# Kept rows turned on VectorE, down weights rounded on ScalarE, and the last 64 features stacked twice

## The reference

```python
s = silu(einsum('bsh,ih->bsi', x, w_gate))
k = int(0.5 * I)                                   # I = 2752
_, idx = jax.lax.top_k(-jnp.abs(s), k)             # the k smallest magnitudes of each row
s[row, idx] = 0
s = s * einsum('bsh,ih->bsi', x, w_up)
return einsum('bsi,hi->bsh', s, w_down)
```

## Time and profile before

| | |
|---|---|
| median of three runs | 1414.09 us (1413.16 to 1414.87) |
| profiled execution | 1414.52 us, span 1412.3 us, mean granted clock 0.99 |
| busy over the span | PE 1367.9 (97%), DVE 981.3 (69%), ACT 739.8 (52%), POOL 942.9 (67%) |
| gate ends, up ends | 851.9 and 1087.8 us |
| down: first matmul, last group from | 1090.9 and about 1280 us |
| chain that ended last | PE 90%, DVE 3%, ACT 2% |

### The profile page before, as it was taken

The page is one execution under the profiler, slowest core; times in us unless marked ns, Lnnn a source line. Parts: engine busy times, 40 slices in busy tenths (PEclk is TensorE's granted clock), DMA queues, the critical chain, the costliest instruction groups (busy, mean ns, idle before and its releaser), DMA issues.

```text
span 1412.3 us, 30485 instructions
## 1 busy us (share of the span) xinstructions
PE 1367.9 (97%) x12727; PEld 1014.2 (72%) x12727; DVE 981.3 (69%) x1324; ACT 739.8 (52%) x935; POOL 942.9 (67%) x613
## 2 busy tenths in 40 slices
PE   4999999999999999899999999999999999999996
PEld 3555555555555555599999998888887888887874
DVE  6888888888888888870001898999997223255654
ACT  6788888888888888732224625243331111111211
POOL 0799888888888888813443342423334899999791
PEclk9899999999999999999999999999999999999998
DMA  9032423233323230024337348383837876865551
GB/s 357 28 103 104 137 98 112 101 115 104 117 100 121 98 107 17 16 77 166 141 123 299 122 163 289 112 286 114 279 120 245 300 256 190 270 191 181 154 192 53
DMA packets 110013, 217.58 MB, mean 154 GB/s; under 512 B 7200, under 2 KB 82864, under 8 KB 104880
## 3 DMA queue, kind: packets, MB, share of 16 engines
q1 hardware_dynamic: 88928, 192.89, 39.6%
q10 hardware_dynamic: 20944, 22.70, 5.2%
HBM read 173.63 MB, written 41.94 MB: 153 GB/s over the span
## 4 chain that ended last, share of the span: by engine, by line
PE 90%; DVE 3%; ACT 2%; DMA 1%; issue 1%; POOL 1%; SPq 0%; DVEq 0%; ACTq 0%; POOLq 0%
PE fast_psum L2002 17%; PE fast_psum L1895 16%; PE fast_psum L2032 15%; PE fast_psum L1913 15%; PE fast_psum L1980 15%; PE fast_psum L1932 6%; PE fast_psum L1939 1%; PE fast_psum L2062 1%; PE fast_psum L2016 1%; PE fast_psum L2083 1%; PE fast_psum L1918 1%; DMA fast_d_raw<-w_down 1%; ACT fast_below L1745 1%; PE fast_psum L1862 1%; ACT fast_g_hi L1717 1%
## 5 line engine op out<-in xcount | busy, mean ns | idle before, releaser
L1321 DVE TENSOR_TENSOR fast_masked<-fast_psum,fast_mask_t 128x1024 f32<-128x1024 f32 (+1 forms) x416 | 488.4, 1219 | 72.2 <-PE fast_psum L1895 70.6
L1177 POOL TENSOR_TENSOR fast_pair<-fast_probs 128x1024 f32<-128x1024 f32 x192 | 457.5, 2386 | 96.1 <-PE fast_psum L1932 47.6
L1658 ACT ACTIVATE fast_probs<-fast_masked 128x1024 f32<-128x1024 f32 (+1 forms) x416 | 438.0, 1058 | 68.6 <-DVE fast_masked L1321 53.6
L1895 PE MATMUL fast_psum<-fast_qT,fast_kraw 32*128 32x256 f32 (+1 forms) x3328 | 247.1, 403 | 6.8 <-ACT fast_qT L1605 3.2
L1913 PE MATMUL fast_psum<-fast_probs,fast_vraw 128*32 128x256 f32 (+1 forms) x3328 | 226.5, 386 | 0.8 <-ACT fast_probs L1658 0.8
L1895 PEld LDWEIGHTS fast_psum<-fast_qT,fast_kraw 32*128 32x128 f32 (+1 forms) x3328 | 153.7, 182 | 93.3 <-DVE fast_masked L1321 53.9
L1232 POOL TENSOR_TENSOR fast_d_lo<-fast_d_raw,fast_d_hi 128x256 fp32r<-128x256 f32 (+1 forms) x264 | 198.4, 781 | 5.3
L1208 POOL TENSOR_TENSOR fast_g_lo<-fast_g_raw,fast_g_hi 128x2816 fp32r<-128x2816 f32 x14 | 87.8, 6273 | 145.6 <-ACT fast_g_hi L1717 123.6
L1980 PE MATMUL fast_psum<-fast_g_hi,fast_z_hi 128*128 128x352 f32 x512 | 165.7, 324 | 1.7 <-POOL fast_g_lo L1208 1.7
L1980 PE MATMUL fast_psum<-fast_g_hi,fast_z_lo 128*128 128x352 f32 x512 | 165.7, 324 | 0.0
L1980 PE MATMUL fast_psum<-fast_g_lo,fast_z_hi 128*128 128x352 f32 x512 | 165.5, 323 | 0.0
(11 more groups left out here) (164 smaller groups left out, 1903.3 us busy)
## 6 DMA issues: line engine op xcount, KB each, us to landing
fast_d_raw<-w_down SPq DMA_DIRECT2D x63, 512.0 KB, 4.0
fast_kraw<-ctx_t SPq DMA_DIRECT2D x32, 800.5 KB, 5.9
fast_vraw<-ctx_nat SPq DMA_DIRECT2D x16, 1536.0 KB
fast_g_raw<-w_gate_up SPq DMA_DIRECT2D x15, 1408.0 KB, 7.3
fast_mag<-s SPq DMA_DIRECT2D x8, 1376.0 KB, 9.8
fast_sx<-s SPq DMA_DIRECT2D x8, 1376.0 KB, 6.7
sk<-fast_sx SPq DMA_DIRECT2D x8, 1376.0 KB, 6.7
fast_u_raw<-w_up_t SPq DMA_DIRECT2D x21, 512.0 KB, 5.0
```

The source lines that it names most:

```text
L1177: pool.tensor_tensor(pair[:, n % PAIR_BUFS], both[:, :, 0, :], both[:, :, 1, :], ALU.add).then_inc(paired, 1)
L1321: dve.tensor_tensor(into, of, m, ALU.add).then_inc(mask_added, 1)
L1658: act.activation(probs[0:r, g % RING, hp * HALF:(hp + 1) * HALF], masked[0:r, h % SLOTS, :], ACT.Exp).then_inc(exp_done, 1)
L1895: last = pe.matmul(scores[0:r, (2 * g + hp) % SLOTS, h % 2, i * 256:(i + 1) * 256], kraw[b % BUFS][q, u, c * P:c * P + r], qT[q, b, u, :], ...
```

## The change

The kept rows are no longer turned by TensorE. VectorE's `keep` writes into `near`, and a new `turn_kept(t)` transposes it in blocks of 32x32 into `sx[t]` (two buffers and, for tile 7, a magnitude buffer). ScalarE's new `store_turned(t)` waits for that and writes the turned blocks with four DMAs to `s_t`, laid out by features; a run there is 32 tokens, 128 bytes. ScalarE's `load_factors(n)` loads from `s_t` and `u_t`, and VectorE's multiply takes both from SBUF. `turn` is gone from TensorE. `near` is held until the transpose is through: `nearest` waits for `sx_turned`. The compares come in two batches of three for each pair.

ScalarE gets the rounding of the down weights, `round_down`: two ahead of the steps, and then `round_down(n + 2)` at the end of stage n. GpSimd keeps the subtraction.

For the last chunk, 64 features, the weights and the factors are loaded twice, on partitions 0 to 63 and 64 to 127. `d_hi` holds the high part on the first half and GpSimd writes the low part over the second, so one matmul over 128 rows makes two products; the third is one of 64 rows.

Core of the diff:

```diff
+        BLK = 32
+        QUARTERS = P // BLK
+        twice = lambda n: n % IC == UF
-        UP_ABS_AT = {6: 4, 12: 5, 19: 6, 25: 7}
-        UP_COUNT_AT = {0: (1, 0), 1: (1, 1), 2: (1, 2), 3: (1, 3), 4: (1, 4), 5: (1, 5),
-                       13: (2, 0), 14: (2, 1), 15: (2, 2), 16: (2, 3), 17: (2, 4), 18: (2, 5),
-                       26: (3, 0), 27: (3, 1), 28: (3, 2), 29: (3, 3), 30: (3, 4), 31: (3, 5)}
+        UP_ABS_AT = {6: 4, 11: 5, 19: 6, 24: 7}
+        UP_COUNT_AT = {0: (1, 0), 2: (1, 3), 12: (2, 0), 14: (2, 3), 25: (3, 0), 27: (3, 3)}
-        UP_SK_AT = {1: 1, 5: 2, 7: 3, 12: 4, 13: 5, 18: 6}
+        UP_SX_AT = {1: 2, 2: 3, 7: 4, 8: 5, 13: 6, 14: 7}
+        GATE_STORE_AT = {62: 0}
+        UP_STORE_AT = {0: 1, 11: 2, 12: 3, 23: 4, 25: 5, 36: 6, 39: 7}
...
             for n in range(STEPS):
-                pool.wait_ge(d_full[j], 16 * (n // DS + 1))
+                pool.wait_ge(d_hi_done, n + 1)
-                pool.tensor_copy(d_hi[j][0:r, :], d_raw[j][0:r, :]).then_inc(d_hi_done, 1)
...
-                    dve.wait_ge(kept, t)
+                    dve.wait_ge(sx_turned, t)
                 done(dve.scalar_tensor_tensor(near, mag[t % MAGS], v, mag[t % MAGS], ALU.is_lt, ALU.mult))
...
-                done(dve.scalar_tensor_tensor(sx, near, thr[:, :], sx, ALU.is_ge, ALU.mult))
+                done(dve.scalar_tensor_tensor(near, near, thr[:, :], sx[t], ALU.is_ge, ALU.mult))
...
+            def turn_kept(t):
+                dve.wait_ge(kept, t + 1)
+                dve.transpose(sx[t], near).then_inc(sx_turned, 1)
...
+            def store_turned(t):
+                act.wait_ge(sx_turned, t + 1)
+                if t == TILES - 1:
+                    act.wait_ge(st_stored[t % 2], 16 * QUARTERS * (t // 2))
+                for q in range(QUARTERS):
+                    act.dma_start(s_t.rearrange("(b r) n -> r b n", r=BLK)[:, :, t * P + q * BLK:t * P + (q + 1) * BLK],
+                                  sx[t][q * BLK:(q + 1) * BLK, :].rearrange("r (b n) -> r b n", n=BLK)
+                                  ).then_inc(st_stored[t % 2], 16)
...
+            def load_factors(n):
                 gi, k = divmod(n, IC)
                 if n >= TURNS:
                     act.wait_ge(h_ready, n - TURNS + 1)
+                if k == 0:
+                    turned = max(GROUPS[gi][-1] + 1, TILES - 2)
+                    for j in range(2):
+                        act.wait_ge(st_stored[j], 16 * QUARTERS * ((turned + 1 - j) // 2))
+                m, t0 = len(GROUPS[gi]), GROUPS[gi][0]
+                act.dma_start(t_s[n % TURNS][0:rows(k), 0:m * P], s_t[k * P:k * P + rows(k), t0 * P:(t0 + m) * P]
+                              ).then_inc(ts_full[n % TURNS], 16)
...
                 if i in UP_ABS_AT:
                     measure(UP_ABS_AT[i])
+                if i in UP_STORE_AT:
+                    store_turned(UP_STORE_AT[i])
                 if i in UP_COUNT_AT:
-                    compare(*UP_COUNT_AT[i])
+                    p, r = UP_COUNT_AT[i]
+                    for r in range(r, r + 3):
+                        compare(p, r)
...
+            def round_down(n):
+                j = n % DS
+                act.wait_ge(d_full[j], 16 * loads(n, DS))
+                if n >= DS:
+                    act.wait_ge(d_done, n + 1 - DS)
+                act.copy(d_hi[j][:, :], d_raw[j][:, :]).then_inc(d_hi_done, 1)
+
+            for n in range(DS - 1):
+                round_down(n)
             for n in range(STEPS):
                 take_high(n)
                 if n + TURNS < STEPS:
-                    load_u(n + TURNS)
-                if n % 2 == 1 and n // 2 + BLOCKS < STEPS // 2:
-                    load_block(n // 2 + BLOCKS)
+                    load_factors(n + TURNS)
...
+                if n + DS - 1 < STEPS:
+                    round_down(n + DS - 1)
...
-            for a, (hp, wp) in enumerate(((h_hi, d_hi), (h_hi, d_lo), (h_lo, d_hi))):
+                products = ((h_hi, d_hi, P), (h_hi, d_lo, P), (h_lo, d_hi, P))
+                if twice(n):
+                    products = ((h_hi, d_hi, P), (h_lo, d_hi, UREST))
```

More of the change, by code:

```diff
@@ L855, in fast, with loads @@
         steps = [0]
+        twice = lambda n: n % IC == UF
+        def loads(n, ring):
+            return sum(2 if twice(m) else 1 for m in range(n % ring, n + 1, ring))
         def u_loads(n):
@@ L1484, in multiply @@
                 gi, k = divmod(n, IC)
-                w, r = len(GROUPS[gi]) * P, rows(k)
-                dve.wait_ge(t_turned, n + 1)
+                w = len(GROUPS[gi]) * P
+                dve.wait_ge(ts_full[n % TURNS], 16 * loads(n, TURNS))
                 if n >= 2:
@@ L1801, in take_high @@
                     act.wait_ge(d_done, n + 1 - HS)
-                act.copy(h_hi[n % HS][0:r, 0:w], t_h[n % 2][0:r, 0:w]).then_inc(h_hi_done, 1)
+                act.copy(h_hi[n % HS][:, 0:w], t_h[n % 2][:, 0:w]).then_inc(h_hi_done, 1)
             def take_zt(t):
@@ L2007, in _ @@
                 up(i)
-            def turn(n):
-                gi, k = divmod(n, IC)
-                q, c = n // 2, n % 2 * P
-                pe.wait_ge(sk_full[q % BLOCKS], 16 * (q // BLOCKS + 1))
-                if n >= 2:
-                    pe.wait_ge(h_ready, n - 1)
-                for i in range(len(GROUPS[gi])):
-                    last = pe.transpose(bank[6 + n % 2][0:rows(k), i * P:(i + 1) * P],
-                                        t_sk[q % BLOCKS][:, i, c:c + rows(k)], eye[:, :])
-                last.then_inc(t_turned, 1)
             def down(n, i):
                 gi, k = divmod(n, IC)
-                r, j, jh = rows(k), n % DS, n % HS
+                j, jh = n % DS, n % HS
                 pe.wait_ge(d_lo_done, n + 1)
```

109 lines of the change are left out of this document (46 added, 63 removed).

## The result

The changed kernel takes 1477.93 us, median of four runs (1471.84 to 1479.24), beside 1414.48 for the kernel before: ratio 1.0445, 95% interval 1.0421 to 1.0469. The profiled execution has a span of 1477.1 us, 64.8 longer. The forecast was 1470, range 1428 to 1530.

A forecast was written before the change was run, and what follows sets the result against it. TensorE was taken to set the time, with VectorE about four us behind in the up stage. From 1414.5 us: + 22 (transposes) + 35 (stores) - 19 (TensorE's work) + 17 (ScalarE's order) = 1469.5, forecast 1470, range 1428 to 1530.

The forecast's parts named there:

- A: Down on TensorE: transposes and the last chunks' third product go, -18.9 us together, all on the path.
- B: Group 2 of down: ScalarE's rounding stands ahead of the factor copies TensorE wants, +17 us, lower bound +5.
- D: Turned-tile stores of 128-byte runs hold ScalarE: 25 us ahead of compares, 10 behind the last store, +35 us.
- 416 descriptor times: One store's four DMAs on ScalarE: total wait for outstanding descriptors; at 20 ns each, a hold of 8.3 us.
- 3 x 8.3: Stores 1, 3 and 5 stand ahead of compares VectorE waits for, each delaying it about 8.3 us: +25.
- rival (2): Short store writes cost 30 to 45 ns a descriptor, holds 12.5 to 19 us; total 1488 to 1550; chance 0.18.
- 9 + 10: From VectorE's last transpose to down's first matmul: 9 us with free issues, 10 more for store 7's held descriptors.
- the limit of about 100 outstanding: DMA issues: an issue is held once about 100 descriptors per DMA engine are outstanding, taken from SyncE's rows.
- C: Eight transposes of about 3.0 us on VectorE in the up stage: VectorE ends near 1104, down starts 22 us later.
- rival (3): VectorE hides the transposes because stretched short operations and `nearest`, some 20 us, go away: 1400 us, chance 0.06.
- the banks hold four items: Up stage: TensorE's waits for copies behind ScalarE's waits cost nothing, since banks let it run four items ahead.
- a sign of being wrong: The prediction fails if VectorE's last transpose ends before 1095, or TensorE's up stage ends late without VectorE.

The follow-up runs named there:

- e9: Kernel before plus only the last 64 features stacked twice, two products in place of three: ratio 0.9994.
- e10: Changed kernel with each store's four DMAs spread over items or stages, compares single, GpSimd rounding the weights of steps 34 to 65: 1412.12 us, ratio 0.9973.
- e5: Changed kernel with the rounding of group 2's down weights (steps 44 to 65) back on GpSimd: 1466.6 us, ratio 1.0363.
- e1: Changed kernel with each store DMA writing 32 runs of 11008 bytes in place of 2752 of 128, rows landing in wrong order: 1444.14 us, ratio 1.0194.
- e11: Changed kernel with only the stores of tiles 0 to 6 spread, one DMA behind each of four items: 1450.23 us, ratio 1.0248.
- e3: Changed kernel with stores in long runs and VectorE's transposes replaced by an operation on one column: 1434.86 us, ratio 1.0128.
- e2: Changed kernel with VectorE's transposes replaced by an operation on one column, rows stored unturned: 1475.64 us, ratio 1.0416.
- e6: e1 with the compares single again, one behind each item, in place of batches of three: 1445.19 us, ratio 1.0212.
- e12: e10 without VectorE's transposes, rows stored unturned, an operation on one column in their place: 1408.9 us, ratio 0.9958.

## Why the prediction was right, and where only its sum was

**The number and the sign.** 1470 was forecast and 1477.9 measured. The start of down was put at 22 + 35 = 57 us later and came 63.0 later; down was put at 17 - 19 = -2 and came at +1.8.

**A, TensorE's work: right in kind, its two terms off in opposite ways.** From down's first matmul to step 44 took 198.8 us before and 188.3 after, 10.5 less. Forecast for these two groups: 11.4 for the transposes and 12 x 0.233 = 2.8 for the products, 14.2. The transposes were worth more: 18 matmuls take 4.13 us in the earlier trace rows itself, so a step's three cost 0.33 us and not 0.26, 14.5 in 44 steps. The products were worth less: the last chunk takes 3.8 to 3.9 us in the changed kernel and in e9 where it took 4.35 before, so about 1 us for two chunks, since matmuls of 128 and of 64 rows alternate there (e9). And the three layer-norm steps of group 1, which I had not priced, take 4.8 back (steps 34 to 44: 44.6 before, 45.7 after, 40.9 by the sum; 42.9 in e10, where GpSimd rounds from step 34): 14.5 + 1 - 4.8 = 10.7.

**B, ScalarE's order in group 2: right in sum, each wait smaller.** Forecast +17; group 2 took 107.9 where it took 97.7, and 4.7 of gain from A lie in it, if A gave there what was forecast: +14.9. The chain of waits at route(4) has TensorE behind ScalarE's take_zt:

```profile
1388.28 2.78 PE fast_psum L2050 x12
...
1392.39 1.07 ACT fast_zt L1827 x2
1393.51 3.01 PE fast_psum L2078 x16
1396.52 2.12 PE fast_psum L2050 x6
```

The longest such wait is 2.5 us where 3.3 was worked out, and all waits for fast_zt and fast_hwt grew by 7.9 + 1.8 = 9.7 us where 15.4 was. The rest came by a way that the forecast had not: matmuls behind a gap are slow, 3.01 us for the 16 of a route where 1.86 is usual and 2.12 for six where 1.39 is, with a granted clock of 0.89 from 1385 to 1400 us (the kernel before has one such place, 0.81 from 1301 to 1310), besides some 2 us at steps 44 to 46. e5 gave 9.3 us of group 2 back; what the rest hangs on was not isolated.

**D, the holds: right in kind, too small in size.** The price of one store was 8.3 us; the first one took 0.37 + 8.21 = 8.6 and the last 8.3, the six between them 9.2 to 15.4. By the prediction's 416 descriptor times that is 20 to 37 ns for one. On VectorE three holds cost 36.8 us where 25 were forecast: the term 3 x 8.3 was the one mis-sized, and what was measured is the lower end of rival (2), 3 x 12.5. Behind the last transpose the guess was good: down's first matmul came 20.7 us later, 9 + 10 were forecast. e1 shows that the short runs are the cause, e11 that it is their issue one close behind another. Whether a short write is slow by itself or by the traffic beside it was not separated, and no run measured the limit of about 100 outstanding; in e10 single issues 5.6 us apart were still held. The 8.3 rests on 20 ns a descriptor and a limit of about 100; the three later issues of the first store took 8.21/3 = 2.74 us for 172 each, 16 ns.

**C, the transposes: the price was right, the account was not.** 3.045 us each where 3.0 was taken. But VectorE, had it not waited for the holds, would have ended at 1133.2 - 36.8 = 1096.4, not 1104. About half of the difference is in waits: the kernel before has 7.7 us of them in the search (3.0 for compares, 2.4 for sums, 2.3 for loads), the changed one 0.5 beside the holds, and the forecast had taken off 4. The other part is rival (3)'s mechanism in small: `nearest`, 3.70 us a piece before, took 3.085. Other operations grew as well as shrank, and all that both kernels have are 2.9 us shorter together. The error of C, some 8 us too long, and that of D, some 12 too short, have opposite signs, and it is luck that the sum came out so well.

**The step that failed** is the one that counts a late up stage of TensorE by itself at nothing, "because the banks hold four items". The prediction named it as a sign of being wrong, and the sign came: TensorE's up stage ended 8.5 us after VectorE's last transpose, at 1141.7, by waits of its own: 27 us for copies behind held stores and behind batches of three compares, 7 for weights, 5 at the start behind tile 0's store. In e3, with VectorE through at 1088.1, it still ended 16 us late. Two chains run side by side there and cross on ScalarE, each nearly as long as the other. Taking away work of VectorE's chain therefore gave less than it is long: the holds 36 of the 46 us expected (e1), the transposes 4 of 23 (e2), both 45 of 61 (e3); batches on top of the first took 13 us out of TensorE's stage and nothing out of the time (e6). The forecast had one chain, VectorE's, and added C and D along it. The sum was right within 8 us since the two chains end nearly together in this kernel, which nothing in the forecast foresaw.

**What the mended version says.** Most of the change's loss was not in its idea. With stores spread, compares single and GpSimd back at the rounding where the experts stand, the same design is 0.27% faster than the kernel before, and the price of the transposes there is some 2 us, hardly more than the noise (e12), with 9 us between this version's start of down and the one before.

**What stays open.** How much of TensorE's waits in the changed kernel comes from SyncE's queue, in which the loads of s wait for the stores, was not isolated. Nor was the reason of the stretched operations on VectorE, or why the up stage of one and the same order differs by some 5 us between executions (e5).

## What to carry to other kernels

Count the descriptors of a DMA for each of the 16 engines before putting it on an engine that computes: four in a row of 172 held the issuing engine 8.3 to 15.4 us, one at a time 0.3 us at best and 4.3 at most (e10), and spreading them was worth 28 us here with the same bytes. Ahead of an in-order engine that serves two others, ask for both what stands behind a wait; two chains of equal length hide part of each other's cost, and an edit to one looks worth less than it is until both are moved. Where a change drops rows from some matmuls of a step, look at the order of shapes: alternation took most of what the missing matmuls gave. A stage's slack is the least of the slacks of all engines that feed it, and a batch of waits spends it at once.
